# A mixture-of-experts block: VectorE's weight low halves moved between the first expert's hidden low halves

## The chip, the cores and the metric

The kernel runs on one core of one Trainium2 chip. The metric is the device time of one launch in microseconds (us). All times of instructions below are from one profiled execution and count from the start of its span.

## The reference, cut to what matters

A transformer block on x (32 batches of 32 tokens of 512, so 1024 tokens): cross attention to a context, a layer that binds and unbinds by Fourier transforms, and a mixture of eight experts. The change touches only the last:

```
logits = xf @ Wg + bg                                  # 1024 x 8
one_hot = one_hot(argmax(logits))                      # each token has one expert
h = gelu(einsum('td,edh->eth', xf, W1))                # 512 -> 2048
y = einsum('eth,ehd->etd', h, W2)                      # 2048 -> 512
out = x + einsum('etd,te->td', y, one_hot)
```

The kernel computes each expert only for the tokens that chose it, at most 160 in a round; with these inputs one round does.

## The kernel before, in words

The five engines run programs written out by hand, each in its own order, and meet at counting semaphores. Float32 values are split into two float16 parts: ScalarE makes the high half (a scaled copy), VectorE the low half (value minus high half), and TensorE multiplies high by high, high by low and low by high.

**Weights.** An expert's weights come in eight pieces of 1 MB (`PIECES`): pieces 0 to 3 are W1, 4 to 7 are W2. SyncE loads a piece into a staging buffer (`load_piece`), ScalarE writes its high half (`piece_hi`, semaphore `e_hi`), VectorE its low half (`piece_lo`, semaphore `e_lo`). The low half is the last reader of the staging buffer, so `e_lo` also tells SyncE that the buffer is free. There are eight staging buffers, but the first expert has only the four at the arena's end (`piece_stage`), because the other four overlap data still in use; pieces 4 to 7 of expert 0 go into the buffers of pieces 0 to 3, and so do pieces 0 to 3 of expert 1 behind them. `e_lo` only counts, so the order of VectorE's low halves is the order in which the counts are reached.

**SyncE's order**, one queue: pieces 0 to 6 of expert 0; the stores of the normalised tokens (`l2_dram`); wait for `e_lo` of 4 (low half 3), load piece 7 of expert 0; store x2 (`x2_dram`, 2 MB); then piece k of expert 1, where k = 0, 1, 2, 3 waits for `e_lo` of 5, 6, 7, 8 (low halves 4, 5, 6, 7 of expert 0), and k = 4 to 7 wait for no further low half.

**Routing.** TensorE gives the logits, VectorE picks the expert of each token and builds a permutation (`slots`), TensorE gathers expert 0's tokens by products with it (`first_gather`, four chunks of 16 products), and VectorE copies each chunk to `xs` (`first_gathered`). The semaphore `xs_done` then lets TensorE begin.

**An expert.** TensorE's inner layer has eight steps k, each of 24 products in two groups (12 for each of two hidden tiles); step k waits for `e_lo` of k//2 + 1 and for the gelu of step k - 4, whose bank it uses. For each step ScalarE does a gelu and the pair's high half, VectorE the pair's low half (`h_lo`). Between them ScalarE makes the high half of pieces 6 and 7 of the same expert behind pairs 0 and 2, and of pieces 0, 1 and 2 of the next behind pairs 3, 5 and 7, then pieces 3, 4, 5. The outer layer has four chunks c of four hidden tiles; chunk c waits for `e_lo` of 5 + c and for the `h_lo` of its tiles (pairs 2c and 2c + 1). Behind chunks 1 and 3 come the small products of the last 32 slots, and in the first expert the transposes of the next expert's tokens stand behind chunk 1. VectorE copies these to `xs` (`gathered`) behind the low halves of the next expert's pieces 0 to 3, and TensorE's next expert waits for that copy. The expert after that is the body of a loop that the change leaves alone.

In the kernel before, VectorE's low halves of expert 0's pieces stand so: piece 3 ahead of the logits, pieces 4 and 5 ahead of the first and third chunk copy, pieces 6 and 7 behind hidden pairs 0 and 2, and expert 1's piece 0 behind pair 3.

Of the kernel before, what the change touches and what calls it, by code (L numbers as in the profile page):

```python
# [26 lines left out]
KC = D // P  # L27
# [35 lines left out]
def perceiver_block(nc, i, out):  # L63
    ctx = ExitStack()
    with ctx:
# [188 lines left out]
        def piece_stage(n, k):  # L254

            return k % 4 if is_first(n) else k
# [361 lines left out]
        def _(act):  # L618
# [140 lines left out]
            def piece_hi(n, k):  # L759

                at = piece_stage(n, k)
                act.wait_ge(s[f"e_landed{at}"], piece_landed(n, k))
                hi(w_hl[k][0], e_stage[at], SG if k < 4 else S2).then_inc(s["e_hi"], 1)
# [15 lines left out]
            for n, (m, c, half) in enumerate(SPEC_ORDER):  # L779
                if n == 6:  # L780
# [3 lines left out]
                             bias=dft_bias[:, c, m:m + 1], scale=1.0 / (SX * SF)).then_inc(s["spec_done"], 1)  # L784
                if n in EARLY_PIECES:
                    piece_hi(0, EARLY_PIECES.index(n))
                if n == 18:
# [62 lines left out]
        def _(dve):  # L850
# [3 lines left out]
            def lo(dst, src, scale, h):  # L854

                return v.scalar_tensor_tensor(dst, src, scale, h, ALU.mult, ALU.subtract)  # L856
# [256 lines left out]
            def piece_lo(n, k):  # L1113
                dve.wait_ge(s["e_hi"], n * 8 + k + 1)
                lo(w_hl[k][1], e_stage[piece_stage(n, k)], SG if k < 4 else S2, w_hl[k][0]).then_inc(s["e_lo"], 1)
# [69 lines left out]
            def l2_lo(t):  # L1185
                dve.wait_ge(s["l2_hi"], t + 1)
                v.tensor_tensor(l2_tile(1, t), l2_f[:, t, :], l2_tile(0, t), ALU.subtract).then_inc(s["l2_lo"], 1)
# [31 lines left out]
            dve.wait_ge(s["l2_lo"], HT + 2)  # L1219
            for t in LN_GROUPS[6]:  # L1220
                l2_lo(t)
            piece_lo(0, 3)


            def by_tile(z):
# [30 lines left out]
            def slots(rank):  # L1256

                for half in range(2):
                    ts = slice(half * HT, (half + 1) * HT)
                    v.tensor_tensor(perm[:, ts], slot_iota.unsqueeze(1).broadcast_to((P, HT, CAP)),  # L1260
                                    rank[:, ts].unsqueeze(2).broadcast_to((P, HT, CAP)), ALU.is_equal
                                    ).then_inc(s["perm_done"], 1)

            def first_gathered(c):

                dve.wait_ge(s["first_ps"], c + 1)
                last = v.tensor_copy(xs[:, :, c, :], FIRST_BANKS[c][:, 0:2 * CAP].rearrange("p (z x) -> p z x", z=2))
                if c % 2:
                    last.then_inc(s["xs_done"], 1)

            def gathered(n):

                dve.wait_ge(s["xt_ps"], n)
                for z in range(2):
                    v.tensor_copy(xs[:, z].rearrange("p c x -> p (c x)"),
                                  (BG, BH)[z][:].bitcast(F16)[:, 0:KC * CAP]).then_inc(s["xs_done"], 1)

            def take_ids(r):

                dve.wait_ge(s["ids_ps"], r + 1)  # L1280
                v.tensor_tensor(ids[0], BH[:, 0:2 * E].rearrange("p (e n) -> p e n", n=2),
                                id_offset.unsqueeze(1).broadcast_to((P, E, 2)), ALU.add)
                v.tensor_tensor(ids[1], BH[0:CB, 2 * E:4 * E].rearrange("p (e n) -> p e n", n=2),
                                id_offset[0:CB].unsqueeze(1).broadcast_to((CB, E, 2)), ALU.add)
                v.scalar_tensor_tensor(quarter_ids, BH[:, 2 * E:4 * E].rearrange("p (e n) -> p e n", n=2), float(KC),
                                       quarter_offset.unsqueeze(1).broadcast_to((P, E, 2)), ALU.mult, ALU.add
                                       ).then_inc(s["ids_done"], 1)

            def rows_out(n):

                dve.wait_ge(s["rows_landed"], n * 32 + 32)
                dve.wait_ge(s["y_main"], n + 1)
                v.scalar_tensor_tensor(y_rows[0], BC[:], 1.0 / (S2 * SH), x2_rows[0], ALU.mult, ALU.add
                                       ).then_inc(s["y_head"], 1)
                dve.wait_ge(s["y_ps"], n * 2 + 2)
                v.scalar_tensor_tensor(y_rows[1], BD[:, 0:P], 1.0 / (S2 * SH), x2_rows[1], ALU.mult, ALU.add  # L1296
                                       ).then_inc(s["y_out"], 1)

            def expert(n, prev=True, nxt=True, first=False):
                if prev:  # L1300
                    rows_out(n - 1)
                for k in range(FC // 2):
                    dve.wait_ge(s["h_hi"], n * 8 + k + 1)
                    v.scalar_tensor_tensor(hid_hl[1][:, 2 * k:2 * k + 2, :], hid_f[k % 4], SH,  # L1304
                                           hid_hl[0][:, 2 * k:2 * k + 2, :], ALU.mult, ALU.subtract
                                           ).then_inc(s["h_lo"], 1)
                    if first and k == 2:
                        take_ids(0)
                    if k == 0:
                        piece_lo(n, PIECES - 2)  # L1310
                    elif k == 2:
                        piece_lo(n, PIECES - 1)
                    elif nxt and k == 3:
                        piece_lo(n + 1, 0)
                if nxt:
                    for k in range(1, 4):
                        piece_lo(n + 1, k)
                if nxt:
                    gathered(n + 1)
                    for k in range(4, PIECES - 2):  # L1320
                        piece_lo(n + 1, k)

            def round_(r, first):
                if first:
                    slots(slot_of[:, :, 0])
                    dve.wait_ge(s["count_ps"], 1)
                    v.reduce_max(most, BE[:, 0:E], AX_X).then_inc(s["chain_dve"], 1)
                    dve.wait_ge(s["chain_dve"], next(chain))
                    v.tensor_scalar(more_rounds, most, float(CAP), None, ALU.is_gt).then_inc(s["routed"], 1)
                    piece_lo(0, 4)  # L1330
                    first_gathered(0)
                    first_gathered(1)
                    piece_lo(0, 5)
                    first_gathered(2)
                    first_gathered(3)
                    slots(own_rank)
                else:
                    slots(own_rank)
                    take_ids(r)
                    for k in range(PIECES - 2):  # L1340
                        piece_lo(r * E, k)
                    gathered(r * E)
                expert(r * E, prev=False, first=first)
                with dve.Fori(1, E - 1) as e:
                    expert(r * E + e)
                expert(r * E + (E - 1), nxt=False)
                rows_out(r * E + (E - 1))

            round_(0, True)
            dve.wait_ge(s["routed"], 1)  # L1350
            with dve.If(dve.value_load(more_rounds[0:1, 0:1], min_val=0, max_val=1) > 0):
                with dve.Fori(1, ROUNDS) as r:

                    v.tensor_scalar(own_rank, own_rank, -float(CAP), None, ALU.add).then_inc(s["ranks_moved"], 1)
                    dve.wait_ge(s["scattered"], r * (32 * E))
                    dve.wait_ge(s["ranks_moved"], r)
                    round_(r, False)
# [379 lines left out]
BIND_PRODUCTS = ((0, 6), (12, 16))  # L1737
UNBIND_PRODUCTS = ((4, 10), (20, 22))
EARLY_PIECES = (1, 7, 13, 19)

LN_GROUPS = [range(HT), range(HT, NT)] * 2 + [range(HT), range(HT, HT + 2), range(HT + 2, NT)]

# [103 lines left out]
```

## Time and profile before

| | us |
|---|---|
| median of 3 runs (lowest, highest) | 812.46 (812.34, 813.0) |
| the profiled execution | 817.21 |
| its span | 815.2 |
| TensorE busy | 778.0 (95%) |
| VectorE busy | 626.1 (77%) |
| ScalarE busy | 468.6 (57%) |
| GpSimd busy | 244.6 (30%) |
| first expert's first product | 580.28 |

The span is the time between the first and last instruction in the profile; the profiled execution's own time lies around it, and the median is of runs without a profile. A busy share is of the whole span. PE is TensorE's products, PEld its weight loads, DVE VectorE, ACT ScalarE, SPq SyncE's queue. L12 is line 12 of the kernel; where a helper records an instruction, the line is the helper's: L856 is every low half (`lo`), L622 every high half (`hi`), L815 the gelu, L1267 the chunk copy, L1304 the low half of a hidden pair, L401 a piece's load.

### The profile page before, as it was taken

The page shows a single profiled execution, that of the slowest core. Times are in us where ns is not written, and L with a number is a line of the kernel's source. Part 1 is how long each engine was busy: PE and PEld are TensorE (multiplying, and loading weights), DVE is VectorE, ACT ScalarE, POOL GpSimd, SP SyncE. Part 2 cuts the span into 40 slices and gives each one's busy share as a digit, 9 for nine tenths or more (in the row PEclk, how much of TensorE's full clock was granted, in tenths as well). Part 3 has the DMA queues.
Part 4 walks back from the last instruction along what each step waited for, and adds up shares of the span by engine and source line. Part 5 has one row for each costly group of instructions (what it writes and reads, how often), then busy time and mean ns, then how long its engine had stood idle before and what let it go on. Part 6 is the DMA issues. An engine that isn't in the chain of part 4 may idle for free.

```text
span 815.2 us, 22075 instructions
## 1 busy us (share of the span) xinstructions
PE 778.0 (95%) x8816; PEld 463.4 (57%) x8816; DVE 626.1 (77%) x984; ACT 468.6 (57%) x838; POOL 244.6 (30%) x411
## 2 busy tenths in 40 slices
PE   4999999999999999999999999996899999999995
PEld 2544455554455554455556544555867866876883
DVE  6857888888887887777668668787787878879770
ACT  2726655657665666654548034237468768756960
POOL 1421444333444333444231200013054332232220
PEclk9999999999999999999999999996899999999998
DMA  9353233443234443233522511103899998998610
GB/s 335 142 188 79 58 93 92 107 106 62 75 86 98 106 107 73 61 89 96 121 55 55 208 52 52 51 1 114 291 370 412 399 345 287 371 345 290 241 32 14
DMA packets 93744, 125.54 MB, mean 154 GB/s; under 512 B 76030, under 2 KB 78910, under 8 KB 82416
## 3 DMA queue, kind: packets, MB, share of 16 engines
q1 hardware_dynamic: 91104, 117.65, 45.2%
q0 software_dynamic: 2576, 7.02, 2.4%
q8 instruction: 43, 0.70, 0.3%
q14 instruction: 21, 0.17, 0.1%
HBM read 100.47 MB, written 6.88 MB: 132 GB/s over the span
## 4 chain that ended last, share of the span: by engine, by line
PE 84%; DVE 9%; ACT 3%; DMA 2%; issue 1%; POOL 0%; POOLq 0%; DVEq 0%; ACTq 0%
PE bank L1368 62%; PE bank L1702 10%; PE bank L1481 4%; PE bank L1674 3%; PE bank L1494 2%; ACT arena L705 2%; DVE arena L1004 2%; DVE arena L856 2%; DVE arena L1010 1%; PE bank L1381 1%; DMA arena<-arena 1%; ACT arena L622 1%; PE bank L1661 1%; DVE arena L1026 1%; DMA arena<-in_x_t 1%
## 5 line engine op out<-in xcount | busy, mean ns | idle before, releaser
L1368 PE MATMUL bank<-arena 128*128 128x160 f16 (+8 forms) x4064 | 588.6, 305 | 8.9 <-DVE arena L856 2.9
L1368 PEld LDWEIGHTS bank<-arena 128*128 128x128 f16 (+3 forms) x4064 | 334.9, 100 | 251.1 <-issue 14.5
L622 ACT ACTIVATE arena<-arena 128x256 f16<-128x256 f32 (+4 forms) x293 | 251.0, 905 | 19.9 <-PE bank L1674 9.0
L856 DVE SCALAR_TENSOR_TENSOR arena<-arena 128x2048 f16<-128x2048 f32 (+2 forms) x95 | 199.5, 2119 | 28.5 <-ACT arena L622 23.4
L622 ACT ACTIVATE arena<-bank 128x512 f16<-128x512 f32 (+1 forms) x175 | 101.2, 586 | 155.6 <-PE bank L1368 124.2
L856 DVE SCALAR_TENSOR_TENSOR arena<-bank,arena 128x512 f16<-128x512 f32 (+1 forms) x174 | 117.7, 685 | 58.1 <-ACT arena L622 54.3
L1702 PE MATMUL bank<-arena 128*128 128x512 f16 x384 | 86.6, 379 | 0.0
L705 ACT ACTIVATE arena<-arena 128x257 f32<-128x257 f32 x128 | 63.6, 499 | 27.0 <-DVE arena L1012 27.0
L504 POOL TENSOR_TENSOR arena<-arena 32x1024 f16<-32x1024 f32 (+1 forms) x16 | 33.0, 2064 | 149.0 <-PE bank L1481 145.4
L1702 PEld LDWEIGHTS bank<-arena 128*128 128x128 f16 x384 | 36.2, 98 | 41.1
L521 POOL COPY arena<-arena 32x256 f16 (+1 forms) x128 | 50.7, 396 | 24.0 <-DVE arena L856 11.8
L815 ACT ACTIVATE arena<-bank 128x320 f32<-128x320 f32 x64 | 27.2, 424 | 51.7 <-PE bank L1368 46.9
L578 POOL DMA_INDIRECT arena<-l_dram,arena x14 | 30.0, 2144 | 83.0 <-PE bank L1661 53.5
L1004 DVE SCALAR_TENSOR_TENSOR arena<-bank,arena 128x257 f32<-128x257 f32 x128 | 53.5, 481 | 0.0
L1026 DVE SCALAR_TENSOR_TENSOR arena<-arena 128x256 f16<-128x256 f32 x128 | 53.2, 476 | 0.0
L1304 DVE SCALAR_TENSOR_TENSOR arena<-arena 128x320 f16<-128x320 f32 x64 | 30.2, 488 | 25.1 <-ACT arena L622 22.2
L783 ACT ACTIVATE arena<-bank,arena 128x512 f32<-128x512 f32 x24 | 16.5, 687 | 46.6 <-PE bank L1368 46.2
L569 POOL DMA_INDIRECT out<-arena x16 | 16.5, 1030 | 87.7 <-DVE arena L1296 67.3
L1010 DVE TENSOR_REDUCE arena<-arena 128x4 f32<-128x1028 f32 x32 | 39.2, 1224 | 1.1
L490 POOL TENSOR_TENSOR arena<-arena 128x256 f16<-128x256 f32 (+1 forms) x64 | 38.0, 614 | 1.2
L450 POOL TENSOR_TENSOR arena<-arena 128x4 f32<-128x4 f32 (+1 forms) x7 | 6.5, 927 | 94.8 <-DVE arena L864 94.7
L1481 PEld LDWEIGHTS bank<-arena 128*64 128x64 f16 x1792 | 30.0, 113 | 7.1 <-issue 6.4
(102 smaller groups left out, 456.6 us busy)
## 6 DMA issues: line engine op xcount, KB each, us to landing
arena<-in_w SPq DMA_DIRECT2D x64, 1024.0 KB, 7.9
arena<-in_ctx_t SPq DMA_DIRECT2D x16, 1024.0 KB, 5.3
arena<-in_awt SPq DMA_DIRECT2D x3, 1024.0 KB, 7.1
l_dram<-arena SPq DMA_DIRECT2D x4, 512.0 KB, 3.6
x_dram<-arena SPq DMA_DIRECT2D x1, 2048.0 KB, 13.2
arena<-in_x_t SPq DMA_DIRECT2D x2, 512.0 KB, 4.5
arena<-in_wq_t SPq DMA_DIRECT2D x1, 1024.0 KB, 6.7
arena<-in_x_t SPq DMA_DIRECT2D x1, 1024.0 KB, 9.0
```

What stands on the lines that cost most here:

```text
L490: g.tensor_tensor(q_bd[n][:, :, b, :].rearrange("p c (r q) -> p c r q", r=2), qT[n][:, :, bass.ds(st * (PB * S) + b * S, S)].unsqueeze(2) ...
L504: g.tensor_tensor(vl_cur[0:LAST_ROWS], vl_all[:, bass.ds(m, 1), :].broadcast_to((LAST_ROWS, PAIRS, P)), diag.unsqueeze(2).broadcast_to((LA ...
L521: g.tensor_copy(attT[n][own, :, bass.ds(m * (PB * S), PB * S)] .rearrange("p c (b q) -> p c b q", b=PB), att_st[n][own, :, :, r % 2, :]).t ...
L622: return a.activation(dst, src, ACT.Copy, scale=scale)
L705: a.activation(sm[:, j, :], sm[:, j, :], ACT.Exp, bias=neg_max[:, j:j + 1], scale=ISD / (SX * SK), accum_out=score_sums[:, j:j + 1]).then_ ...
L856: return v.scalar_tensor_tensor(dst, src, scale, h, ALU.mult, ALU.subtract)
L1004: v.scalar_tensor_tensor(sm[:, j, :], bank[:, 0:L], bank[:, L:L + 1], mask_bias, ALU.add, ALU.add).then_inc(s["s_free"], 1)
L1010: v.reduce_max(row_max[:, js], sm[:, js, :], AX_X).then_inc(s["s_max"], 1)
L1026: v.scalar_tensor_tensor(p_hl[1][b][:, j - b * KC, :], sm[:, j, 0:LM], recip[:, j:j + 1], p_hl[0][b][:, j - b * KC, :], ALU.mult, ALU.subtract
L1368: last = m.matmul(out_ap, w, x, start=(n == 0), stop=(n == len(pairs) - 1))
L1481: last = m.matmul(BG[own, cols], w[:, own], x[:, at * HALF:(at + 1) * HALF], start=(n == 0), stop=(n == len(pairs) - 1))
L1702: last = m.matmul(BC[:], hid_hl[z][:, f, 0:P], w[u][:, g, :], start=(f == 0 and u + z == 0), stop=(f == FC - 1 and z == 1))
```

## The change

In the first expert only, VectorE's order changes. The low halves of pieces 3, 4 and 5 leave the routing stage, so the four chunk copies follow each other. The low halves of pieces 3 to 7 come behind the hidden low halves of pairs 0, 2, 4, 6 and 7. The low half of expert 1's piece 0, which stood behind pair 3, comes behind all of these. No other engine's program is changed.

```diff
             for t in LN_GROUPS[6]:
                 l2_lo(t)
-            piece_lo(0, 3)
...
                     if first and k == 2:
                         take_ids(0)
-                    if k == 0:
+                    if first:
+                        if k in FIRST_PIECES:
+                            piece_lo(0, 3 + FIRST_PIECES.index(k))
+                    elif k == 0:
                         piece_lo(n, PIECES - 2)
                     elif k == 2:
                         piece_lo(n, PIECES - 1)
                     elif nxt and k == 3:
                         piece_lo(n + 1, 0)
                 if nxt:
-                    for k in range(1, 4):
+                    for k in range(0 if first else 1, 4):
                         piece_lo(n + 1, k)
...
-                    piece_lo(0, 4)
-                    first_gathered(0)
-                    first_gathered(1)
-                    piece_lo(0, 5)
-                    first_gathered(2)
-                    first_gathered(3)
+                    for c in range(KC):
+                        first_gathered(c)
                     slots(own_rank)
...
+FIRST_PIECES = (0, 2, 4, 6, 7)
```

## Rows read from the trace of the kernel before

**Rows 1.** The page's slices: TensorE's busy tenths in 40 slices of the span.
```profile
PE   4999999999999999999999999996899999999995
```
**Rows 2.** Timeline of TensorE: start, us, engine, line, operation, count [idle before, releaser].
```profile
572.25 7.43 PE L1368 MATMUL bank<-arena 128*128 128x160 f16 x64 [1.96 <-DVE arena L1260]
580.28 14.39 PE L1368 MATMUL bank<-arena 128*128 128x160 f16 x232 [0.60 <-DVE arena L1267]
594.51 5.34 PE L1702 MATMUL bank<-arena 128*128 128x512 f16 x24
599.79 1.52 PE L1674 MATMUL bank<-arena 128*32 128x128 f16 x96
601.24 0.91 PE L1661 MATMUL bank<-arena 128*128 128x128 f16 x16
...
608.83 6.78 PE L1368 MATMUL bank<-arena 128*128 128x160 f16 x91
...
638.15 2.04 PE L1368 MATMUL bank<-arena 128*128 128x160 f16 x27
...
779.83 13.45 PE L1368 MATMUL bank<-arena 128*128 128x160 f16 x192
```
**Rows 3.** The chain that ended last, 577 to 580 us: start, us, what.
```profile
577.23 2.20 DVE arena L856
579.42 0.81 DVE arena L1267 x2
```
**Rows 4.** Timeline of VectorE, routing stage and first hidden pair.
```profile
565.26 2.28 DVE L856 SCALAR_TENSOR_TENSOR arena<-arena 128x2048 f16<-128x2048 f32 x1
568.07 0.23 DVE L1232 SCALAR_TENSOR_TENSOR arena<-bank,arena 128x64 f32<-128x64 f32 x1 [0.52 <-PE bank L1368]
...
576.74 0.49 DVE L1267 CAST arena<-bank 128x320 f16<-128x320 f32 x1 [1.64 <-PE bank L1368]
...
579.34 0.88 DVE L1267 CAST arena<-bank 128x320 f16<-128x320 f32 x2
...
583.12 0.49 DVE L1304 SCALAR_TENSOR_TENSOR arena<-arena 128x320 f16<-128x320 f32 x1 [1.43 <-ACT arena L622]
```
**Rows 5.** Timeline of SyncE's queue: three loads of weight pieces.
```profile
567.57 0.35 SPq L401 DMA_DIRECT2D arena<-in_w  x1
...
574.68 0.35 SPq L401 DMA_DIRECT2D arena<-in_w  x1
...
587.25 0.33 SPq L401 DMA_DIRECT2D arena<-in_w  x1
```
**Rows 6.** DMA traffic of 587 to 592 us in 40 slices.
```profile
GB/s 0 0 0 0 0 0 0 0 0 459 328 262 0 0 66 66 66 197 262 328 393 131 393 590 197 590 328 524 393 328 655 197 590 393 262 262 197 66 0 0
```
**Rows 7.** ScalarE: timeline at pair 2, then groups by form, 583 to 600 us.
```profile
586.88 2.27 ACT L622 ACTIVATE arena<-arena 128x320 f16<-128x320 f32 x2
...
L622 ACT ACTIVATE arena<-arena 128x2048 f16<-128x2048 f32 x6 | 11.3, 1895 | 0.0
L622 ACT ACTIVATE arena<-arena 128x320 f16<-128x320 f32 x8 | 3.8, 470 | 0.3
L815 ACT ACTIVATE arena<-bank 128x320 f32<-128x320 f32 x7 | 3.0, 422 | 0.7 <-PE bank L1368 0.7
```
**Rows 8.** Windows: length, busy us of five engines (count), granted clock, DMA share, GB/s.
```profile
557.00:572.00 15.00, 6.65 (x108) 5.69 (x108) 12.03 (x26) 12.47 (x14) 3.02 (x3) 0.52 0.43 128
572.00:578.00 6.00, 5.75 (x44) 5.76 (x45) 4.32 (x7) 0.39 (x1) 0.00 (x0) 0.50 0.99 341
578.00:582.00 4.00, 3.40 (x48) 3.20 (x46) 3.69 (x5) 0.00 (x0) 0.00 (x0) 0.98 1.07 422
...
810.00:815.00 5.00, 0.00 (x0) 0.00 (x0) 0.00 (x0) 0.00 (x0) 0.00 (x0) 0.53 0.01 3
```
**Rows 9.** DMA view, 575 to 577.9 us: packets by size.
```profile
DMA packets 529, 1.10 MB, mean 379 GB/s; under 512 B 0, under 2 KB 0, under 8 KB 528
```
**Rows 10.** The page's DMA issues: context loads, count, KB each, median us to landing.
```profile
arena<-in_ctx_t SPq DMA_DIRECT2D x16, 1024.0 KB, 5.3
```

## The prediction

> **What bounds the kernel now.** I read the page's slices first, then the order of TensorE's work, then the chain of the end, then who releases whom around the change. In the slices TensorE is the busy engine throughout, with one dip at the routing stage before the first expert [rows 1]. From 580.28 us on it works nearly without a gap: the first expert is 14.39 us of inner products, two outer halves of 5.34 us with their small products and transposes, and the second expert's inner products begin at 608.83; the last expert's start at 779.83 [rows 2]. So every microsecond that TensorE is made to wait behind 580 us moves the end, unless it waited there already, and it didn't.
>
> The chain ahead of 580.28 runs through VectorE: gather products, a chunk copy, the low half of piece 5 (2.20 us at 577.23), two copies, first inner product [rows 3]. That looks like time to win. But the 64 gather products run from 572.25 for 7.43 us, to 579.68 [rows 2], and the last copy can't start before that. Two copies take 0.88 us from 579.34 [rows 4], the second starting near 579.8.
>
> **What the change wins.** Piece 3's low half stood at 565.26 to 567.54, and VectorE then still waited 0.52 us for the logits, which TensorE had to give [rows 4]: taking it away frees nothing. Piece 4's delayed only the first copy; the second copy, at 576.74, came after 1.64 us of waiting for TensorE [rows 4]. Piece 5's delayed the third copy by some 0.8 us, but the fourth at most by 579.8 - 579.7 = 0.1 us. Gain: 0.0 to 0.1 us; I take 0.1. If the modelled end of the products were late by the whole overlap, it would be at most 2.2 us. Nothing else is saved: the same instructions run in another order.
>
> **What it delays: the weight queue.** The low halves do more than feed TensorE. Each frees a staging buffer, and SyncE issues in order: piece 7 of expert 0 after low half 3, then the 2 MB store of x2, then pieces 0, 1, 2 and 3 of expert 1 after low halves 4, 5, 6, 7. SyncE issued piece 7 at 567.57, 0.03 us after low half 3 ended (565.26 + 2.28), and expert 1's first piece at 574.68, its third at 587.25 [rows 4, 5]. ScalarE is in order as well: it must make the high half of piece 7 between hidden pairs 2 and 3, expert 1's piece 0 after pair 3, piece 1 after pair 5. In the kernel before these weights had long landed. Now the low half that frees the buffer stands behind a hidden pair that stands behind the landing of the load before it. That is a ring: VectorE low half, load, ScalarE high half, gelu, VectorE hidden low half, next low half.
>
> Prices of a turn. A load alone: issued 587.25, the last slice with traffic is the 38th of 40 in 587 to 592, thus landed at 591.6, 4.4 us [rows 5, 6]. The piece's high half on ScalarE 1.91 us [rows 7]; gelu and the pair's high half 0.42 + 0.47 = 0.9 us [rows 7]; the pair's low half 0.49, or 0.45 with the next behind it, and a piece's low half 2.2 us back to back [rows 3, 4]. The turn, in times of the profiled run:
> - Pair 0's low half ends at 583.6 (583.12 + 0.49 [rows 4]), low half 3 at 585.8. Piece 7 is issued then and lands at 585.9 + 4.4 = 590.3. ScalarE was ready at 587.35 (586.88 + 0.47 [rows 7]) and is held 3 us; its high half ends 592.2, pair 3's gelu at 592.6, just before TensorE wants that bank (its eighth inner step starts about 580.28 + 7/8 of 14.39 = 592.9). No loss yet.
> - Pair 2's low half and the ids end at 588.3, low half 4 at 590.5. Expert 1's piece 0 is issued, but behind the x2 store, itself behind piece 7. Store: 2.10 MB at the 341 GB/s of 572 to 578, 6.15 us; piece 0 behind it 1.05 MB at the 422 GB/s of 578 to 582, 2.5 us [rows 8]. Landed 590.3 + 6.15 + 2.5 = 598.9. High half to 600.8, pair 4 to 601.7, its low half to 602.2, low half 5 at 604.4. TensorE needs low half 5 for the second outer chunk, at 594.51 + 2.7 = 597.2. It waits 7.2 us.
> - Piece 1 issued 604.4, landed 608.8; high half to 610.7, pair 6 to 611.6, its low half to 612.0, low half 6 at 614.3. TensorE resumed at 604.4, has 2.7 + 1.5 + 0.9 = 5.1 us of work [rows 2] to 609.5, waits 4.8 us. Pair 7's low half and low half 7 end at 616.9. The last two outer chunks and their small products: 614.3 + 2.7 + 2.7 + 1.45 = 621.1, against 608.83 before: 12.3 us.
> - Expert 1's inputs are copied behind its first four low halves. VectorE: 616.9 + 4 x 2.2 + 0.9 = 626.6. ScalarE fits beside it: piece 3 issued 616.9, landed 621.3, high half 623.2, low half 625.4. TensorE starts expert 1 at 626.6, against 608.83: **17.8 us**, of which the last 5.5 us are this wait.
>
> After that the loads run freely: expert 1's piece 7 lands about 616.9 + 4.4 + 4 x 2.5 = 631.3 and expert 2's pieces every 2.5 us, some 8 us less ahead of TensorE than now, still before their use (expert 2 would start near 655). Expert 1 takes TensorE 638.15 - 608.83 = 29.3 us, the five behind it (779.83 - 638.15) / 5 = 28.3 each [rows 2], so their order should hold, and about 1 us could come back.
>
> **The queue's order.** The trace shows a load issued at 574.68 that has none of its 8 KB packets among the 528 of 575 to 577.9, all of them the store's 2 KB ones [rows 9]: it stands behind the store. The Trainium skill, DMA: Bandwidth & Descriptors, section Queues, rings and completion order, says each engine consumes descriptors in ring order, and the trace agrees; that speaks against this change. The same page (its section on two DMAs through one engine) says completion isn't ordered. If piece 0 overtook the store, it would land 590.5 + 4.4 = 594.9, 4.0 us earlier, and the sum would be 13.8 us. That is my lower term.
>
> **The clock.** In 557 to 572 TensorE was busy 6.65 of 15 us and had a granted clock of 0.52; in 572 to 578, busy without pause, still 0.50; in 578 to 582 it had 0.98. Behind the last product, in 810 to 815, it was 0.53 [rows 8]. New waits of 7.2, 4.8 and 5.5 us are like these. At 1.2 GHz a 160-column product took 131 ns (5.75 us / 44 [rows 8]), at 2.4 GHz 70 ns (13.45 / 192 [rows 2]), so a stretch at the low level loses half of itself. Low stretches inside the first expert are hidden by the waits behind them; the one at expert 1's start isn't: 0 to 6 us at the low level costs 0 to 3 us, and one behind the second wait up to 2 more. I take 2. The Trainium skill, TensorE: Matmul & The Clock Gate, section HAM oscillation, says that waits for data throttle the engine anew each time; by it the sum would be 22 us or more, without it 17.7.
>
> **Sum.** -0.1 + 17.8 + 2.0 = 19.7 us. The profiled run took 817.21 us, its span is 815.2, the median of the timed runs 812.46; the difference carries over unchanged, so 812.46 + 19.7 = 832.2, given as 832.0.
>
> **Rivals.**
> - Piece 0 overtakes the store, or the latencies are shorter, and the clock stays up: 812.46 + 13.8 = 826.3. For it: completions may overlap. Against: rows 9. Chance 0.15.
> - More is lost: every load takes the 5.3 us of the context loads [rows 10] rather than 4.4 (three in the ring, 2.7 us), the clock costs 5, and expert 2 waits for weights, since the lead is 8 us shorter: 2 or 3 us more. 812.46 + 17.8 + 2.7 + 5 + 2 = 840. Chance 0.10.
> - Faster: the low half of piece 5 was truly on the path, and the ring is covered. It gives up to 2.2 us, 810.3. It decides only if piece 7 and expert 1's first pieces land before ScalarE comes to them, thus within about 1.5 us of issue for piece 7 (587.35 - 585.9); rows 6 say 4.4. Chance 0.02.
> - Nothing: only ScalarE waits, and TensorE's bank lead covers it. That needs low half 5 before 597.2, while it comes behind pair 4. Chance 0.03.
> - The forecast: 0.70.
>
> **Range.** Low: 13.8, less the 1 us that could come back, 825.3, given as 825.0. High: 17.8 + 2.7 + 5 + 1 = 26.5, 839. Changes below 0.2% (1.6 us) can hardly be told from none. Faster 0.02, same 0.03, slower 0.95.
>
> **What would show it.** SyncE's load of piece 7 issued near 586 rather than 567.6, the store behind it; ScalarE waiting for a load before pairs 3, 4 and 6; TensorE with three gaps, between the first and second outer chunk, between the second and third, and ahead of expert 1's first product, behind VectorE's piece low halves and the copies; granted clock below 1 in 600 to 630; from expert 2 on the same lengths as before. It is wrong if the first outer half stays whole, if the store's packets come after piece 0's, or if later experts show gaps or get shorter.

## The result, and the profile after

| | before | after |
|---|---|---|
| median of the timed runs, us | 812.40 (4 runs) | 836.41 (4 runs, 834.28 to 837.49) |
| span of the profiled execution | 815.2, in a second one 810.0 | 833.6 |
| VectorE busy | 626.1 | 626.0 |
| TensorE busy | 778.0, in the second 772.6 | 779.8 |

The changed kernel is slower: ratio 1.0291, 95% interval 1.0279 to 1.0303, 24.0 us. Forecast were 19.7 us more, given as 832.0, in a range of 825 to 839. No engine gets more work: TensorE has 8816 products in either kernel. Against the second profile of before it sits idle 16.4 us longer (53.8 against 37.4) and is busy 7.2 us longer, since some products run at the lower clock. Most of this stands in the first expert. TensorE's timeline of the changed kernel (start, us, engine, line, count, and in brackets the idle time before it with its releaser; TensorE's lines are two lower than in [rows 2], so L1366 is L1368 there, and VectorE's L1266, L1274 and L1303 are L1267, L1275 and L1304 of the kernel before):

```profile
571.86 6.73 PE L1366 MATMUL bank<-arena 128*128 128x160 f16 x64 [1.96 <-DVE arena L1259]
579.18 12.73 PE L1366 MATMUL bank<-arena 128*128 128x160 f16 x208 [0.58 <-DVE arena L1266]
593.72 1.82 PE L1366 MATMUL bank<-arena 128*128 128x160 f16 x24 [1.80 <-ACT arena L815]
595.37 2.75 PE L1700 MATMUL bank<-arena 128*128 128x512 f16 x12
606.03 4.93 PE L1700 MATMUL bank<-arena 128*128 128x512 f16 x12 [7.91 <-DVE arena L856]
610.90 1.52 PE L1672 MATMUL bank<-arena 128*32 128x128 f16 x96
612.35 0.91 PE L1659 MATMUL bank<-arena 128*128 128x128 f16 x16
616.45 7.04 PE L1700 MATMUL bank<-arena 128*128 128x512 f16 x24 [3.18 <-DVE arena L856]
623.42 1.52 PE L1672 MATMUL bank<-arena 128*32 128x128 f16 x96
629.40 15.82 PE L1366 MATMUL bank<-arena 128*128 128x160 f16 x192 [4.46 <-DVE arena L1274]
...
659.37 13.45 PE L1366 MATMUL bank<-arena 128*128 128x160 f16 x192
...
797.95 13.45 PE L1366 MATMUL bank<-arena 128*128 128x160 f16 x192
```

Four waits where [rows 2] have none: 1.80 us at the eighth inner step for a gelu, 7.91 and 3.18 us at the second and third outer chunk for VectorE's low halves (L856), 4.46 us ahead of expert 1 for its inputs. What stands behind them is on ScalarE, whose high halves of pieces (128x2048) now wait for DMA:

```profile
591.34 1.91 ACT L622 ACTIVATE arena<-arena 128x2048 f16<-128x2048 f32 x1 [5.08 <-DMA arena<-in_w]
593.15 0.42 ACT L815 ACTIVATE arena<-bank 128x320 f32<-128x320 f32 x1
...
600.51 1.91 ACT L622 ACTIVATE arena<-arena 128x2048 f16<-128x2048 f32 x1 [6.44 <-DMA arena<-in_w]
...
610.93 1.91 ACT L622 ACTIVATE arena<-arena 128x2048 f16<-128x2048 f32 x1 [6.86 <-DMA arena<-in_w]
...
621.69 1.91 ACT L622 ACTIVATE arena<-arena 128x2048 f16<-128x2048 f32 x1 [7.20 <-DMA arena<-in_w]
```

These are piece 7 of expert 0 and pieces 0, 1 and 2 of expert 1. In the kernel before, piece 7 and piece 0 followed the high halves of their pairs at once: the 2.27 us row of [rows 7] holds pair 2 and piece 7 with nothing between, and this one of the same profile pair 3 and piece 0:

```profile
589.51 2.27 ACT L622 ACTIVATE arena<-arena 128x320 f16<-128x320 f32 x2
```

SyncE's queue shows why; its loads answer to [rows 5]:

```profile
584.74 0.34 SPq L401 DMA_DIRECT2D arena<-in_w  x1
585.13 0.43 SPq L417 DMA_DIRECT2D x_dram<-arena  x1
589.24 0.34 SPq L401 DMA_DIRECT2D arena<-in_w  x1
```

Piece 7 leaves at 584.74 instead of 567.57, expert 1's piece 0 at 589.24 instead of 574.68. VectorE's side closes the ring (L1303 is the low half of a hidden pair, here pair 4):

```profile
603.28 0.49 DVE L1303 SCALAR_TENSOR_TENSOR arena<-arena 128x320 f16<-128x320 f32 x1 [8.68 <-ACT arena L622]
```

Low half 5 stands behind pair 4, which waited 8.68 us for ScalarE, which waited for piece 0, which SyncE could issue only when low half 4 had ended. The chain that ended last shows the whole way (start, us, what):

```profile
587.01 2.21 DVE arena L856
...
589.24 11.25 DMA arena<-in_w
...
603.28 0.49 DVE arena L1303
603.77 2.21 DVE arena L856
...
606.00 4.90 DMA arena<-in_w
...
616.79 2.21 DVE arena L856
...
619.02 5.27 DMA arena<-in_w
...
626.25 2.29 DVE arena L856
628.55 0.81 DVE arena L1274 x2
```

It goes from low half 4 to piece 0 of expert 1, by pair 4 to low half 5, to piece 1, by pair 6 to low half 6, by pair 7 to low half 7, to piece 3, and by its low half to the copies of expert 1's tokens. Piece 2 isn't on it.

### The profile page after: what moved, and what is told of

It reads as the page before. It is cut to its first block, busy times and chain, and to the rows that moved or that the text cites. A ratio compares the mean times of both kernels' runs of the same rounds, so it can differ in the third digit from the quotient of the medians.

```text
span 833.6 us, 22075 instructions
## 1 busy us (share of the span) xinstructions
PE 779.8 (94%) x8816; PEld 464.9 (56%) x8816; DVE 626.0 (75%) x984; ACT 468.1 (56%) x838; POOL 238.1 (29%) x411
## 4 chain that ended last, share of the span: by engine, by line
PE 78%; DVE 11%; DMA 4%; ACT 3%; issue 1%; SPq 1%; POOL 0%; POOLq 0%; DVEq 0%; ACTq 0%
PE bank L1366 60%; PE bank L1700 9%; PE bank L1479 3%; DVE arena L856 3%; DMA arena<-in_w 3%; PE bank L1492 2%; PE bank L1672 2%; ACT arena L705 2%; DVE arena L1004 2%; ACT arena L622 1%; DVE arena L1010 1%; DMA arena<-arena 1%; DMA arena<-in_mask 1%; DVE arena L1026 1%; PE bank L1659 1%
## 5 line engine op out<-in xcount | busy, mean ns | idle before, releaser
L1366 PE MATMUL bank<-arena 128*128 128x160 f16 (+8 forms) x4064 | 589.7, 306 | 15.6 <-DVE arena L1274 4.5
L1366 PEld LDWEIGHTS bank<-arena 128*128 128x128 f16 (+3 forms) x4064 | 336.3, 100 | 257.4 <-issue 15.0
L856 DVE SCALAR_TENSOR_TENSOR arena<-arena 128x2048 f16<-128x2048 f32 (+2 forms) x95 | 200.0, 2124 | 22.2 <-ACT arena L622 22.0
L856 DVE SCALAR_TENSOR_TENSOR arena<-bank,arena 128x512 f16<-128x512 f32 (+1 forms) x174 | 117.7, 684 | 58.0 <-ACT arena L622 54.2
L1700 PE MATMUL bank<-arena 128*128 128x512 f16 x384 | 90.6, 392 | 11.1 <-DVE arena L856 11.1
L1303 DVE SCALAR_TENSOR_TENSOR arena<-arena 128x320 f16<-128x320 f32 x64 | 30.0, 487 | 44.2 <-ACT arena L622 44.2
L578 POOL DMA_INDIRECT arena<-l_dram,arena x14 | 23.9, 1710 | 85.2 <-PE bank L1659 56.5
L569 POOL DMA_INDIRECT out<-arena x16 | 17.8, 1113 | 102.5 <-DVE arena L1295 82.1
```

What stands on the lines that cost most here:

```text
L1366: last = m.matmul(out_ap, w, x, start=(n == 0), stop=(n == len(pairs) - 1))
L1700: last = m.matmul(BC[:], hid_hl[z][:, f, 0:P], w[u][:, g, :], start=(f == 0 and u + z == 0), stop=(f == FC - 1 and z == 1))
```

## Experiments

The theory is the ring: a low half frees a buffer, the load lands, ScalarE makes its high half and only then the gelu behind it, and the next low half stands behind that gelu's pair. The rivals: the late loads are the bound whatever ScalarE does; the store doesn't matter; the copies were on the path; any delay of low halves costs its length. The median of before in the shared runs is 812.2 to 812.7.

### The kernel before once more

No edit.

> The kernel before once more, unchanged, for a second profile. Its first profiled execution took 817.2 us against 812.4 to 812.7 in the timed runs, and in it experts 1 to 6 took 28.3 to 29.3 us of TensorE where those of the other kernels' profiles take 27.6. If those 3 to 5 us are chance of that one execution (TensorE's short stops between products), this profile has a span near 810.5 and experts of 27.6 us. If a profile always costs this kernel 4.8 us, the span is near 815 again.

Measured: 812.01, span 810.0. So the first profile's 815.2 was chance of one execution. TensorE's timeline:

```profile
572.60 6.39 PE L1368 MATMUL bank<-arena 128*128 128x160 f16 x64 [1.96 <-DVE arena L1260]
580.36 14.39 PE L1368 MATMUL bank<-arena 128*128 128x160 f16 x232 [1.37 <-DVE arena L1267]
...
608.91 13.45 PE L1368 MATMUL bank<-arena 128*128 128x160 f16 x192
...
636.52 13.45 PE L1368 MATMUL bank<-arena 128*128 128x160 f16 x192
...
774.57 13.45 PE L1368 MATMUL bank<-arena 128*128 128x160 f16 x192
```

Each expert takes 27.61 us (636.52 - 608.91), without the short stops that the first profile had in them (29.3 and 28.3 us from [rows 2]). This profile is the one to compare with, since its span and the timed runs agree: 833.6 - 810.0 = 23.6 us against the 24.0 measured. The first would have explained only 18.4.

### ScalarE's order opened

The changed kernel, and in ScalarE's first expert:

```diff
...
-                    elif nxt and k % 2 and k > 1:
+                    elif nxt and k % 2 and k > 1 and not first:
                         piece_hi(n + 1, k // 2 - 1)
+                if first:
+                    for k in range(3):
+                        piece_hi(n + 1, k)
```

> The changed kernel with ScalarE's order changed in the first expert alone: the high halves of expert 1's pieces 0, 1 and 2 stand behind pair 7 and not behind pairs 3, 5 and 7. This opens the ring: a gelu no longer stands behind a load of expert 1. Ring theory: TensorE's waits at the second and third outer chunk vanish (the 1.8 us at the eighth inner step stays, it hangs on expert 0's piece 7), the first expert ends near 610, and only expert 1's inputs come late, first product near 613.5 against 607.7 for the kernel before counted from the same start: 818 to 820. Rival, that the loads themselves are the bound, late by their release from low halves 4 to 7 whatever ScalarE does: 834 to 836.

Measured: 822.15, ratio 1.0110 (1.0093 to 1.0127): 14.3 of the 24.0 us are back, with VectorE's and SyncE's programs as in the changed kernel. TensorE waits no more at the outer chunks:

```profile
580.61 12.73 PE L1369 MATMUL bank<-arena 128*128 128x160 f16 x208 [0.58 <-DVE arena L1269]
595.31 3.21 PE L1369 MATMUL bank<-arena 128*128 128x160 f16 x24 [1.96 <-ACT arena L815]
598.31 5.64 PE L1703 MATMUL bank<-arena 128*128 128x512 f16 x24
...
617.21 16.13 PE L1369 MATMUL bank<-arena 128*128 128x160 f16 x192 [4.22 <-DVE arena L1277]
```

The rival of the loads as the only bound (834 to 836) is out. Expected were 818 to 820, 2 to 4 us less. The profile shows two parts of that. Expert 1's first product came 36.6 us after the first expert's (617.21 - 580.61) where 34.3 were expected; the chain that ended last has a load of 7.25 us there, piece 3 from issue to landing, where the changed kernel took 5.27. And expert 1's inner products took 16.13 us at the lower clock instead of 13.45, which the expectation doesn't name. The eighth step was slow too (3.21 instead of 1.82), but the wait of 4.22 us behind it took that in.

### The store out of the ring

The changed kernel, and in SyncE's order:

```diff
-            sp.wait_ge(s["e_lo"], PIECES - 4)
-            load_piece(0, 0, PIECES - 1)
             sp.wait_ge(s["x2_done"], NT)
             sp.dma_start(i["x2_dram"]...
+            sp.wait_ge(s["e_lo"], PIECES - 4)
+            load_piece(0, 0, PIECES - 1)
```

> The changed kernel with SyncE's 2 MB store of x2 ahead of piece 7's load and its wait, so the store leaves near 566 us and is out of the ring. Ring theory with a queue in order: expert 1's piece 0, issued near 589, lands after 4.4 to 5 us instead of 11.3, first product of expert 1 7 to 8 us earlier: 829. It also tells why piece 7 took 6.6 us from issue to ScalarE's start instead of 4.4: if the store issued 0.4 us behind it slowed it, it takes 4.4 to 4.9 here; if a cold queue did, 6.6 again. Rival, that loads pass the store in the queue: 836.

Measured: 831.06, 5.4 us back of 7 to 8 expected. ScalarE's timeline of this kernel:

```profile
589.81 1.91 ACT L622 ACTIVATE arena<-arena 128x2048 f16<-128x2048 f32 x1 [3.37 <-DMA arena<-in_w]
...
595.36 1.91 ACT L622 ACTIVATE arena<-arena 128x2048 f16<-128x2048 f32 x1 [2.82 <-DMA arena<-in_w]
```

Both loads were issued at the times of the changed kernel (584.93 and 589.4), but piece 7 landed in 4.8 us where it had taken 6.6, and piece 0 was used at 595.4 instead of 600.5. So the store cost piece 7 1.8 us and piece 0 5.1 us. Some 0.9 us is lost again ahead of expert 1: the third outer chunk begins 5.5 us earlier than in the changed kernel, counted from the first expert's start, but expert 1 only 4.6 us (45.65 instead of 50.22), because piece 3 took 6.15 us from issue to landing instead of 5.27. Why, stays open.

### Piece 3 ahead of the logits again

```diff
                 l2_lo(t)
+            piece_lo(0, 3)
...
-                            piece_lo(0, 3 + FIRST_PIECES.index(k))
+                            piece_lo(0, 4 + FIRST_PIECES.index(k))
...
-FIRST_PIECES = (0, 2, 4, 6, 7)
+FIRST_PIECES = (2, 4, 6, 7)
```

> The changed kernel with one part undone: piece 3's low half is back ahead of the logits; 4, 5, 6 and 7 stay behind pairs 2, 4, 6 and 7. Piece 7's load and the 2 MB store of x2 are then issued near 566 us. Ring theory: ScalarE isn't held before pair 3; expert 1's piece 0 is issued near 589.3 behind nothing and lands 4.4 to 5 us later, near 594, its high half to 596, pair 4 to 597, low half 5 to 599.5, two more links as in the changed kernel, expert 1's first product near 622 instead of 629.4: 836.4 - 7.5 = 829. Rival, that the store and piece 7 don't matter and only VectorE's order behind the pairs does: 836. Rival, that the delay all begins with piece 3: 812 to 815.

Measured: 831.70, ratio 1.0225 (1.0208 to 1.0242), 4.7 us back. The store and piece 7 are early here too; that neither kernel gets below 831 says that the ring through pieces 0, 1 and 3 of expert 1 turns on without them. Expected were 829. Piece 0 took 6.4 us to ScalarE's start (issued 589.55, used 596.01), more than the 4.4 to 5 expected; why, stays open.

### Both undone

The changed kernel with ScalarE's order opened and piece 3 early.

> The changed kernel with piece 3's low half back ahead of the logits and ScalarE's high halves of expert 1's pieces 0 to 2 behind pair 7: both closures of the ring are open, only low halves 4 to 7 still come late. Ring theory: no wait inside the first expert, which ends 27.9 to 28.6 us after its start; expert 1's piece 3 is issued near 601, its low half ends near 610, first product of expert 1 near 611 to 612, some 3 us late: 815.5 to 817. If the two undone parts overlap in what they give back (4.7 and 14.3 us alone, together 19.0 of 24.0), the remainder is 5 us: 817.5. If the low halves' place alone costs more than that: 820 or more.

Measured: 817.64, ratio 1.0059 (1.0044 to 1.0073). This is the sum of the two (14.3 + 4.7 = 19.0 of 24.0, rest 5.0) nearly to the number: 5.4 us over the before of these runs. One wait is left, ahead of expert 1:

```profile
611.60 14.75 PE L1370 MATMUL bank<-arena 128*128 128x160 f16 x192 [3.60 <-DVE arena L1278]
```

3.60 us of waiting and 14.75 - 13.45 = 1.3 us of slower products make 4.9.

### The four copies together, without late weights

The kernel before, with pieces 4 and 5 behind the permutation of the other experts:

```diff
-                    piece_lo(0, 4)
-                    first_gathered(0)
-                    first_gathered(1)
-                    piece_lo(0, 5)
-                    first_gathered(2)
-                    first_gathered(3)
+                    for c in range(KC):
+                        first_gathered(c)
                     slots(own_rank)
+                    piece_lo(0, 4)
+                    piece_lo(0, 5)
```

> The kernel before with the change's first half alone: the four chunk copies follow each other, and the low halves of pieces 4 and 5 stand behind the permutation of the other experts, ahead of hidden pair 0; piece 3 stays ahead of the logits, 6 and 7 behind pairs 0 and 2. Ring theory (the loss comes from loads that wait for low halves that wait for hidden pairs): the copies gain at most 0.1 us because the fourth waits for TensorE either way, and loads of expert 1 come 5 to 8 us later than before but ahead of ScalarE, so 812.4, within 0.5 us, and the fourth copy still waits for TensorE. Rival, that the copies were on the path: the first expert starts up to 2.2 us earlier, 810.2. Rival, that any delay of the low halves costs its own length: 814 to 817.

Measured: 816.82, ratio 1.0047 (1.0030 to 1.0063), 4.1 us slower. Here my expectation failed: the copies cost nothing, but the rest did. The profile has a wait that no list of mine had:

```profile
599.83 1.52 PE L1672 MATMUL bank<-arena 128*32 128x128 f16 x96
604.08 0.91 PE L1659 MATMUL bank<-arena 128*128 128x128 f16 x16 [2.73 <-DMA arena<-l_dram,arena]
604.92 7.04 PE L1700 MATMUL bank<-arena 128*128 128x512 f16 x24
```

TensorE waits 2.73 us for the gathered tokens of expert 1, and the outer half behind it takes 7.04 instead of 5.34 us at a lower clock: 4.4 us.

### The same, with the ids at their old time

```diff
                     if first and k == 2:
                         take_ids(0)
-                    if k == 0:
+                    if first and k == 0:
+                        piece_lo(0, 5)
+                    elif first and k == 2:
+                        piece_lo(0, 6)
+                        piece_lo(0, 7)
+                    elif k == 0:
...
+                    for c in range(KC):
+                        first_gathered(c)
+                    slots(own_rank)
                     piece_lo(0, 4)
...
```

> The four copies together as in the first experiment, but the token ids of the other experts taken as early as in the kernel before: low half 4 behind the permutation, 5 behind pair 0, 6 and 7 behind the ids at pair 2. The first experiment lost 4.1 us with one wait of 2.7 us for the gathered tokens of expert 1, whose ids came 1.5 us later. If the late ids were the cause, this is 812.5 to 813. If it was the traffic of the weight loads, which are issued in a heap beside the token gather in both kernels, there is again a wait of 2 to 3 us ahead of the token transposes: 815 to 817.

Measured: 816.77. The ids aren't the cause. GpSimd's gathers show it; first this kernel, then the kernel before (second profile):

```profile
588.76 7.86 POOL L578 DMA_INDIRECT arena<-l_dram,arena  x1 [26.35 <-issue]
596.93 0.88 POOL L578 DMA_INDIRECT arena<-l_dram,arena  x1 [0.30 <-issue]
```
```profile
589.37 3.27 POOL L578 DMA_INDIRECT arena<-l_dram,arena  x1 [27.07 <-issue]
592.94 2.00 POOL L578 DMA_INDIRECT arena<-l_dram,arena  x1 [0.30 <-issue]
```

The first gather began 0.6 us earlier and took 7.86 us instead of 3.27. In 589 to 601 us the DMA moved 363 GB/s here and 336 in the first profile of before. That the weight loads beside it hold the gather up fits both kernels; that it is their traffic, and not their place in the queue, wasn't separated.

### TensorE kept busy in its waits

The changed kernel, with products that nobody reads ahead of three waits (32, 18 and 20 of 480 columns):

```diff
+                    if first and c in (1, 2):
+                        keep_busy((0, 32, 18)[c], (None, BG, BA)[c], ...)
                     pe.wait_ge(s["e_lo"], n * 8 + 5 + c)
```

> The changed kernel with products that nobody reads put into three of TensorE's waits in the first expert: 32 ahead of the second outer chunk, 18 ahead of the third, 20 ahead of expert 1 (480 columns each, about 0.2 us at full clock), into free banks. They fill the waits of 7.9, 3.2 and 4.5 us without reaching past them. If the clock's part of the loss is as the changed kernel's profile shows it (expert 1's inner products 15.8 instead of 13.45 us; what is slow inside the first expert hides in the next wait), this gives back 2.4 us: 834. If the clock stays low anyway, 836.4; if the products delay the real ones, more than 837.

Measured: 836.93, no gain. The second outer chunk ran at full clock, as did the third and fourth, but the clock fell in what was left of the last wait:

```profile
617.15 5.37 PE L1707 MATMUL bank<-arena 128*128 128x512 f16 x24 [1.56 <-DVE arena L856]
...
623.91 4.22 PE L1581 MATMUL bank<-arena 128*128 128x480 f16 x20
631.06 14.98 PE L1366 MATMUL bank<-arena 128*128 128x160 f16 x192 [2.93 <-DVE arena L1274]
```

Expert 1's products took 14.98 instead of 15.82 us, 0.8 back, while its inputs came 51.47 us after the first expert's start (631.06 - 579.59) instead of 50.22. Expert 1's piece 3 was used 1.3 us later here, counted from the first expert's start (46.4 us after it instead of 45.1); why, stays open. That what is slow inside the first expert costs nothing fits this run, since 5.37 instead of 7.04 us there brought expert 1 no earlier, but with piece 3 later as well the run doesn't show it alone.

### Piece 5 alone, and the routing stage kept busy

Three kernels on the kernel before. The first moves low half 5 behind the permutation and leaves all else:

```diff
-                    piece_lo(0, 5)
                     first_gathered(2)
                     first_gathered(3)
                     slots(own_rank)
+                    piece_lo(0, 5)
```

> The kernel before with the low half of piece 5 alone moved, from between the second and third chunk copy to behind the permutation of the other experts; piece 4 stays ahead of the copies, everything else as before. The second profile of the kernel before shows 1.37 us between the last gather product and the first expert (the clock had risen earlier), the first shows 0.60. If low half 5 is on the path by that difference, this gains 0.4 to 0.8 us: 812.0. Expert 1's piece 1 is loaded 2 to 3 us later, in a stretch without other loads, so the token gather shouldn't suffer. If it does as in the two kernels with all copies together: 815 to 817.

Measured: 812.26 against 812.24, ratio 1.0003 (0.9994 to 1.0011): nothing, within 0.5 us of gain and 0.9 of loss. So the rival that any delay of a low half costs its length is out for this one. The second leaves VectorE's order and puts unread products (8, 6, 6 and 7 of 512 columns) into TensorE's gaps ahead of the gate's transposes, the onehot wait and the gather products.

> The kernel before with products that nobody reads in four gaps of TensorE in the routing stage (8 and 6 between the gate's transposes, 6 ahead of the onehot wait, 7 ahead of the gather products; 512 columns). The order of VectorE is that of the kernel before. If the clock stays at full, the 64 gather products take 4.5 us instead of 7.4, and the copies and low half 5 then end about 1.6 us earlier: 811. Then piece 5's low half would truly stand on the path. If the clock falls all the same, each of the extra products takes 0.43 us and some reach past their gaps: 813 to 815.

Measured: 811.73, ratio 0.9988 (0.9978 to 0.9997). The third does both.

> The same with the unread products of the busy-routing kernel in TensorE's gaps. There the gather products took 4.59 us and TensorE then waited 1.37 us for the copies behind low half 5. Here the wait falls to 0.6 us, since the last copy follows its product: 0.8 us less than that kernel's 811.7, thus 810.9, and 1.7 us less than before. If the token gather is hit by the loads: 814.

Measured: 810.06, ratio 0.9971 (0.9960 to 0.9982), 2.2 us faster than before and the largest gain here. TensorE of the second, then of the third kernel:

```profile
572.37 4.59 PE L1368 MATMUL bank<-arena 128*128 128x160 f16 x64
578.33 14.39 PE L1368 MATMUL bank<-arena 128*128 128x160 f16 x232 [1.37 <-DVE arena L1267]
```
```profile
573.48 4.59 PE L1368 MATMUL bank<-arena 128*128 128x160 f16 x64
578.65 14.39 PE L1368 MATMUL bank<-arena 128*128 128x160 f16 x232 [0.58 <-DVE arena L1267]
```

The gather products took 4.59 us instead of 6.4 to 7.4, and with them that fast low half 5 is on the path by 1.37 - 0.58 = 0.8 us. When they take 7.4 us, TensorE itself is late enough to cover it (0.60 in [rows 2]); in the second profile of the kernel before they took 6.39, and the wait was 1.37 as well. That the third kernel gains over the second by this 0.8 us isn't shown by the two profiles: the third's gather products began 1.1 us later, its first expert no earlier (578.65 against 578.33), and the spans are 809.0 and 809.1.

## Why the prediction was right, and where its terms were off

The 23.6 us between the two spans (810.0 and 833.6), by the starts shown above:

| stretch | before, us | after, us | difference |
|---|---|---|---|
| to the first gather product | 572.60 | 571.86 | -0.7 |
| gather products and copies, to the first expert | 7.76 | 7.32 | -0.4 |
| first expert, to expert 1's start | 28.55 | 50.22 | +21.7 |
| expert 1 | 27.61 | 29.97 | +2.4 |
| experts 2 to 6 | 138.05 | 138.58 | +0.5 |
| expert 7 to the end | 35.43 | 35.65 | +0.2 |

**The copies.** Forecast -0.1, measured -0.4 here; the move of low half 5 alone is within noise. The step was right for the profile that it was read from, where the fourth copy waits for TensorE. It isn't always so: the gather products took 7.43, 6.39 and 7.42 us in three profiles of the old order or nearly so, and in the one of 6.39 low half 5 held the last copy up by 0.8 us. The 0.7 us ahead of them isn't the change's: three other profiles with piece 3's low half moved have the first gather product at 572.67 to 572.74, against 572.60 before.

**The ring.** Forecast 17.8, measured 21.7; the mechanism is shown by the opened kernels (14.3, 5.4 and 4.7 us back) and by the chain that ended last. The term mis-sized is the landing of the loads: the three on that chain, pieces 0, 1 and 3 of expert 1, were put at 8.4, 4.4 and 4.4 us and took 11.25, 4.90 and 5.27, in sum 4.2 us more. My times, less the 1.1 us by which the changed kernel's profile starts its first expert earlier than the first profile of before, against the trace:

| step | forecast | measured |
|---|---|---|
| low half 3 ends | 584.7 | 584.7 |
| piece 7 used by ScalarE | 589.2 | 591.3 |
| low half 4 ends | 589.4 | 589.2 |
| piece 0 of expert 1 used | 597.8 | 600.5 |
| low half 5 ends | 603.3 | 606.0 |
| piece 1 used | 607.7 | 610.9 |
| low half 6 ends | 613.2 | 616.4 |
| low half 7 ends | 615.8 | 618.9 |
| expert 1 starts | 625.5 | 629.4 |

Piece 7 took 6.6 us instead of 4.4, as the store was issued 0.4 us behind it (4.8 without it). Store and piece 0 then took 9.2 us (591.3 to 600.5) where I had 8.65, and the loads behind them 4.9 to 5.3 instead of 4.4: I had read the landing from the slices with traffic, 4.4 us, and left out what lies between the last of them and the semaphore. The rival "more is lost" had 5.3 us for every load, and in that part it came nearer than the forecast; its 5 us for the clock and its late weights of expert 2 did not come. The result lies in the range because its upper end had that rival's loads and clock in it. The wait of 1.8 us at the eighth inner step, which I had as "no loss yet" with 0.3 us to spare, came with piece 7's delay; it cost nothing in the end, as the wait of 7.91 us behind it took it in.

**The queue's order.** Right: the store landed at 598.1 us and piece 0 behind it at 600.4 (11.2 us from issue to landing), and taking the store away gave 5.4 us. The rival of 826.3 falls.

**The clock.** Forecast 2, measured 2.4 (15.82 against 13.45 us in expert 1). The granted clock was 0.50 in 601 to 610, in 618 to 620 and in 628 to 634 us and 1.00 between; what was slow in the outer chunks fell into the waits behind them, as forecast. By the Trainium skill's rule (TensorE: Matmul & The Clock Gate, section HAM oscillation) I had 22 us or more for the sum, and 24.0 were measured. The trace agrees that the clock fell anew behind waits, three times, but the 2.4 us are near my own term, and the rest of the extra is of the loads.

**Given back.** I had about 1 us, of expert 1's 29.3. Against the first profile far more came back: 3.1 us in experts 2 to 6 (27.7 us each instead of 28.3) and, the slow products set aside, 1.7 in expert 1; against the second profile nothing did. The difference was in the profile of before, not in the change: that execution took 4.8 us more than its median (817.21 to 812.46), while the changed kernel's took 0.8 less (835.64 to 836.41). The sum stood only because it was built from steps inside the first expert, where both profiles of before agree (28.55 us to expert 1).

## What to carry to other kernels

A copy that is the last reader of a buffer is a link of the load behind it: before moving it, follow the buffer's next load through its queue to the instruction that waits for it, and look whether that engine, in order, holds up the very work that the copy now stands behind. If it does, each turn costs the load's whole latency and what stands between: here 10.4 us from the end of low half 5 to that of low half 6, 4.9 of them the load. Work that looks free to move because its consumer is late may still be early for the queue, and a large store in that queue belongs ahead of the waits, not behind them (here 5.4 us). One profile can be 5 us off its kernel's timed runs; take a second before its lengths go into a table.

## What the runs showed of the hardware

- A 1 MB load issued 0.4 us ahead of a 2 MB store in the same queue landed in 6.6 us; alone in 4.8. In the changed kernel and the two with an early store, the other loads on the chain that stood behind no store took 4.8 to 6.4 us.
- The span of GpSimd's indirect gather on its engine went from 3.27 to 7.86 us when more weight loads ran beside it (310 GB/s in 589 to 594 us instead of 251 to 254), and was 5.66 us in the kernel with the four copies together.
- TensorE's clock came back behind 578 us in one profile of the kernel before [rows 8] and in 576 to 578 in the other, with the same work ahead of it, so the same 64 products took 7.43 or 6.39 us. The windows of the second profile (length, busy us of five engines, granted clock, DMA share, GB/s):

```profile
572.00:576.00 4.00, 3.40 (x26) 3.40 (x27) 3.41 (x5) 0.74 (x1) 0.00 (x0) 0.50 0.94 309
576.00:578.00 2.00, 2.00 (x28) 2.00 (x27) 1.18 (x2) 0.00 (x0) 0.00 (x0) 0.91 1.07 388
```

- The same kernel's profiled execution had a span of 815.2 us once and 810.0 another time; experts 1 to 6 took 5.3 us longer there. Seven stops of TensorE of 0.2 to 0.4 us for which the trace names no releaser make 2.1 us of it; the rest lies inside rows that took longer for the same products. The cause stays open.
